# Second attention of a decoder layer: scores and contexts of two batches at once, as 64 by 64 products on quarters of the TensorE array

## What is computed

```python
x = x + xattn(layernorm(x), ctx_512)          # ctx_512: (32, 64, 64)

kv_r   = rope(kv_c)                           # (b, 64 keys, 64)
q_big  = rope(einsum('bshk,hkq->bshq', q, w_kc_q))
q_r    = einsum('bshq,hqr->bhsr', q_big, W_qr)
k_r    = einsum('bld,hdr->bhlr', kv_r, W_kr)
scores = einsum('bhsr,bhlr->bhsl', q_r, k_r)  # 16 heads, 64 by 64
attn   = softmax(scores)
ctx_c  = einsum('bhsl,bld->bhsd', attn, kv_r)
ctx    = einsum('bhsd,hkd->bhsk', ctx_c, w_kc_kv)
return ctx.reshape(b, s, H * K) @ Wo.T
```

## Time and profile before

| | us |
|---|---|
| median of 3 runs | 771.22 |
| the three runs | 771.22, 772.04, 767.51 |
| the profiled execution, in all | 763.03 |
| its span in the trace | 761.2 |
| mean granted clock of PE, as a share of full | 0.955 |

### The profile page before, as it was taken

How to read it: one execution, slowest core, us unless ns; L and a number is a source line. 1 busy time by engine, 2 the same in 40 slices (tenths; PEclk the granted TensorE clock), 3 DMA queues, 4 the chain that set the end, 5 groups by cost and what they waited for, 6 DMA issues and landing times.

```text
span 761.2 us, 13640 instructions
## 1 busy us (share of the span) xinstructions
PE 662.7 (87%) x4850; PEld 490.5 (64%) x4850; DVE 529.0 (69%) x1237; ACT 333.4 (44%) x1001; POOL 237.2 (31%) x219
## 2 busy tenths in 40 slices
PE   4787999989999889989899898998979797899780
PEld 2465777767785557856578465785656586788660
DVE  4998789994676868578794777846587746344472
ACT  0477789986721173011730117301366354444340
POOL 1131000000028423453446534465334001201554
PEclk9997899996999999999999999999999999999995
DMA  8799800000000000000000100001071133333545
GB/s 302 162 382 420 351 2 2 1 2 1 2 15 15 1 1 1 1 14 1 16 21 23 55 1 15 22 21 43 14 251 50 48 93 97 117 105 100 155 127 179
DMA packets 49905, 61.44 MB, mean 81 GB/s; under 512 B 15536, under 2 KB 42416, under 8 KB 49584
## 3 DMA queue, kind: packets, MB, share of 16 engines
q1 hardware_dynamic: 45104, 50.88, 20.1%
q0 software_dynamic: 3072, 8.39, 3.6%
q10 hardware_dynamic: 1664, 1.31, 0.6%
HBM read 29.37 MB, written 31.20 MB: 80 GB/s over the span
## 4 chain that ended last, share of the span: by engine, by line
PE 65%; DVE 14%; ACT 9%; issue 6%; POOL 3%; DMA 2%; another core or an unknown queue 1%; ACTq 0%; POOLq 0%; DVEq 0%
PE bank L348 55%; PE bank L357 9%; DVE m L1052 3%; ACT ex L1546 2%; POOL r L1701 2%; ACT kbd L1425 1%; DVE qmax L1264 1%; DVE wlo L1296 1%; ACT vbd L1411 1%; DMA lncol<-in_L_attn_ln_kv_b 1%; DVE csum L1273 1%; POOL gb L1753 1%; ACT ex L1435 1%; ACT xth L1391 1%
## 5 line engine op out<-in xcount | busy, mean ns | idle before, releaser
L1052 DVE TENSOR_TENSOR m<-bank,cst 128x512 f32<-128x512 f32 x192 | 118.8, 682 | 47.0 <-PE bank L348 46.2
L1701 POOL TENSOR_TENSOR r<-m,m 128x512 f32<-128x512 f32 x72 | 91.3, 1291 | 134.9 <-DVE m L1052 123.0
L348 PE MATMUL bank<-xth,wbh 128*128 128x512 f32 x192 | 83.4, 434 | 4.1 <-DVE m L1052 4.1
L348 PE MATMUL bank<-xth,wbl 128*128 128x512 f32 x192 | 75.1, 391 | 0.0
L348 PE MATMUL bank<-xtl,wbh 128*128 128x512 f32 x192 | 75.1, 391 | 0.0
L1534 ACT ACTIVATE qc<-bank 128x512 f32<-128x512 f32 x32 | 17.4, 595 | 128.8 <-PE bank L348 128.8
L1546 ACT ACTIVATE ex<-bank,nmax 128x64 f32<-128x64 f32 x256 | 56.1, 346 | 27.2 <-DVE nmax L1267 27.0
L348 PE MATMUL bank<-r,wqk 64*64 64x512 f32 x512 | 61.1, 621 | 1.7 <-POOL r L1701 1.7
L1721 POOL TENSOR_TENSOR ex<-ex,inv 128x512 f32<-128x512 f32 x32 | 33.3, 1042 | 82.7 <-DVE inv L1276 82.5
L348 PE MATMUL bank<-wop,qc 128*128 128x256 f32 x256 | 58.0, 379 | 0.6 <-DVE qc L1281 0.6
L348 PEld LDWEIGHTS bank<-wop,qc 128*128 128x128 f32 x256 | 48.5, 190 | 11.4 <-issue 4.3
(11 more groups left out here) (218 smaller groups left out, 1553.4 us busy)
## 6 DMA issues: line engine op xcount, KB each, us to landing
slots<-cst SPq DMA_DIRECT2D x1, 13312.0 KB, 44.2
xs<-slots SPq DMA_DIRECT2D x46, 128.0 KB
slots<-ys SPq DMA_DIRECT2D x46, 128.0 KB
slots<-cst SPq DMA_DIRECT2D x1, 5120.0 KB, 49.7
wo_s<-in_L_xattn_Wo SPq DMA_DIRECT2D x1, 2048.0 KB, 18.3
wq_s<-in_L_xattn_Wq SPq DMA_DIRECT2D x1, 2048.0 KB, 11.9
wraw<-in_L_ffn_Wg SPq DMA_DIRECT2D x8, 256.0 KB, 5.0
wraw<-in_L_ffn_Wu SPq DMA_DIRECT2D x8, 256.0 KB, 5.3
```

The costliest lines, as they stand in the source:

```text
L348: return e.matmul(o, l, r, start=start, stop=stop, skip_group_check=True)
L1052: last = e.tensor_tensor(m4[n % 2][m][:, :].rearrange("p (b s) -> p b s", s=S), products[half][:, :].rearrange("p (b s) -> p b s", s=S), t ...
L1701: last = e.tensor_tensor(rope[n % 6][half][:, :], m4[n % 2][first][:, :], m4[n % 2][second][:, :], op)
```

## The change

Scores. The block-diagonal keys are gone. POOL writes the rotated context straight into `kvr[blk % 2]` (two buffers now, 128 partitions by 8 batches by 64, the same 64 rows twice), and `context_T` turns it into `kvT` by 16 products with the identity, 64 by 64 by 64, once per block at n = 9, with one copy of 128x512 on ACT. `cross_scores` now makes two batches in 32 products of 64 by 64 by 64, each on a quarter of the array, into banks 4 and 5: heads with even number within `qc` rows 0 to 63 go to bank 4, the others to bank 5. So each bank holds half the heads of both batches; maximum, exponentials, sum, normalisation and transposes go on as before, eight times per block, on a bank each.

Contexts. Instead of one product of 128 by 128 by 512, `contexts` makes four of 64 by 64 by 256, for half the heads of two batches, into `context_banks`, banks 1 and 7. Both calls of a pair have to be done before DVE can copy a batch out, so `context_out` runs twice in steps 5, 7, 9 and 11. The heads end in a new order, which is made good by folding the output weights in that order (`context_head`, `outputs_T`, `outputs_fold`).

Banks. Since bank 1 now holds contexts and bank 3 the output products, the six tiles ahead all use banks 0 and 2, and tile n waits for c_rm of 12 blk + n, that is for DVE's products of tile n-1. The seventh tile waits for the last context copy and the last addition to x of the block before.

Order. `cross_scores` comes at s = 0, 2, 4, 6 at the head of the step; `AHEAD` moves the first three tiles one step forward; `norm_T` does two at a time at s = 0 and 1; `cross_out` comes at s = 7, 9, 11, 12.

```diff
-        AHEAD = {5: 0, 6: 1, 7: 2, 8: 3, 10: 4, 12: 5}
+        AHEAD = {4: 0, 5: 1, 6: 2, 8: 3, 10: 4, 12: 5}
...
-        out_bank = lambda blk, t: bank[4 + t % 2 if blk < 3 else t]
-        OUT_AT = [{9: 0, 10: 1, 11: 2, 12: 3}] * 3 + [{6: 0, 8: 1, 10: 2, 12: 3}]
+        out_bank = lambda blk, t: bank[3] if blk < 3 else bank[(0, 2, 3, 4)[t]]
+        OUT_AT = {7: 0, 9: 1, 11: 2, 12: 3}
+        context_banks = (bank[1], bank[7])
...
-            odd = (n + (blk == 0)) % 2
+            odd = 0 if blk and n < 6 else (n + 1) % 2
             return bank[odd], bank[2 + odd]
...
-                w.wait_ge(c_rm, 12 * blk + n - 1 if n > 1 else 12 * blk)
+                if blk and n < 6:
+                    w.wait_ge(c_rm, 12 * blk + n)
+                elif blk and n == 6:
+                    w.wait_ge(c_cn, 8 * blk)
+                    w.wait_ge(c_xc, 4 * blk)
+                else:
+                    w.wait_ge(c_rm, 12 * blk + n - 1 if n > 1 else 0)
...
-            def cross_scores(blk, b):
-                i = 8 * blk + b
+            def cross_scores(blk, d):
+
+                i = 8 * blk + 2 * d
                 w.wait_ge(c_qb, 8 * blk + 6)
-                w.wait_ge(c_kvT, 2 * (blk + 1))
-                w.wait_ge(s_ex, 32 + i - 1)
-                for n in range(NP):
-                    if n == 6:
+                w.wait_ge(c_kvT, blk + 1)
+                w.wait_ge(s_ex, 32 + i)
+                for n2 in range(4):
+                    if n2 == 3:
                         w.wait_ge(c_qb, 8 * (blk + 1))
-                    at = 64 * (n % 2)
-                    last = mm(e, bank[4 + b % 2][at:at + 64, (n // 2) * P:(n // 2 + 1) * P], qc[:, n, b * 64:(b + 1) * 64], kvbdT[:, b, :], True, True)
-                last.then_inc(s_S, 1)
+                    for b2 in range(2):
+                        b, at = 2 * d + b2, 256 * b2 + 64 * (n2 ^ b2)
+                        for odd in range(2):
+                            rows = slice(64 * odd, 64 * odd + 64)
+                            for c in range(2):
+                                last = mm(e, bank[4 + odd][64 * c:64 * c + 64, at:at + 64], qc[rows, 2 * n2 + c, b * 64:(b + 1) * 64], kvT[rows, b, :], True, True)
+                last.then_inc(s_S, 2)
...
             def contexts(blk, b):
                 i = 8 * blk + b
+                d, u = divmod(b, 2)
                 w.wait_ge(s_exs, 32 + i + 1)
-                w.wait_ge(c_cn, i)
+                w.wait_ge(c_cn, 8 * blk + 2 * d)
                 w.wait_ge(r_route, RK * blk)
-                mm(e, bank[7][:, :], kvbd[:, b, :], ssb[b % 2][:, :], True, True).then_inc(c_ctxv, 1)
+                for b2 in range(2):
+                    for s in range(2):
+                        rows, c = slice(64 * s, 64 * s + 64), s ^ b2
+                        last = mm(e, context_banks[b2][64 * c:64 * c + 64, 256 * u:256 * u + 256], kvr[blk % 2][rows, 2 * d + b2, :],
+                                  ssb[b % 2][rows, 256 * b2:256 * b2 + 256], True, True)
+                last.then_inc(c_ctxv, 1)
...
             def context_out(blk, b):
-                i = 8 * blk + b
-                w.wait_ge(c_ctxv, i + 1)
-                e.tensor_copy(qc[:, :, b * 64:(b + 1) * 64], bank[7][:, :].rearrange("p (n s) -> p n s", s=S)).then_inc(c_cn, 1)
+                w.wait_ge(c_ctxv, 8 * blk + b + 2 - b % 2)
+                e.tensor_copy(qc[:, :, b * 64:(b + 1) * 64], context_banks[b % 2][:, :].rearrange("p (n s) -> p n s", s=S)).then_inc(c_cn, 1)
...
-                    if 4 <= s < 12:
-                        context_out(blk, s - 4)
-                    if 1 <= s < 5 and blk < 3:
-                        norm_T(blk, s - 1)
-                    if s - 1 in OUT_AT[blk]:
-                        cross_out(blk, OUT_AT[blk][s - 1])
+                    if 5 <= s < 12 and s % 2:
+                        for b in (s - 5, s - 4):
+                            context_out(blk, b)
+                    if 1 <= s < 3 and blk < 3:
+                        for m in (2 * s - 2, 2 * s - 1):
+                            norm_T(blk, m)
+                    if s - 1 in OUT_AT:
+                        cross_out(blk, OUT_AT[s - 1])
...
-            def context_diag(blk):
-                w.wait_ge(c_kvr, blk + 1)
-                w.wait_ge(s_S, 16)
-                w.wait_ge(c_ctxv, 8 * blk)
-                w.wait_ge(c_kvTp, 2 * blk)
-                for h2 in range(2):
-                    last = e.tensor_tensor(kvbd[:, :, 64 * h2:64 * h2 + 64], kvr[:, :, :],
-                                           C("half")[:, h2:h2 + 1].rearrange("p (o d) -> p o d", o=1).broadcast_to([P, 8, XC]), ALU.mult)
-                last.then_inc(c_kvbd, 1)
```

More of the change, by code:

```diff
@@ L607, in outputs_T @@
                 w.wait_ge(s_oT, n)
-                transposes(e, [(bank[3][:, (h * 2 + t) * P:(h * 2 + t + 1) * P], wo_s[:, t, (2 * n + h) * P:(2 * n + h + 1) * P])
-                               for h in range(2) for t in range(2)]).then_inc(s_oTp, 1)
+                at = lambda s: P * context_head(n // 2, n % 2, s)
+                transposes(e, [(bank[3][:, (s * 2 + t) * P:(s * 2 + t + 1) * P], wo_s[:, t, at(s):at(s) + P])
+                               for s in range(2) for t in range(2)]).then_inc(s_oTp, 1)
             def outputs_fold(g):
@@ L1559, in norm_T @@
                 w.wait_ge(c_proj, 24 * (blk + 1))
-                e.activation(xth[:, k, 256 * half:256 * half + 256], bank[m % 2][:, 0:256], ACT.Copy).then_inc(s_xth, 1)
+                e.activation(xth[:, k, 256 * half:256 * half + 256], bank[2 * (m % 2)][:, 0:256], ACT.Copy).then_inc(s_xth, 1)
             def weights_high(n):
```

93 lines of the change are left out of this document (50 added, 43 removed).

## The result

The changed kernel took 815.2 us (median of four runs, 809.6 to 816.7) against 769.4 for the kernel before in the same session: a ratio of 1.0565, 95% interval 1.0496 to 1.0634, or 46 us more. The forecast was 23.6 us more, and 815.2 lies above its range. The profiled execution took 809.63 us, with a span of 807.8 (before: 761.2).

The account below looks back on a forecast made before the run. PE was taken to bound part two's second stretch, the scores-to-exponentials loop its first. The sum 5.3 + 2 x 6.4 - 0.5 + 6.0 = 23.6 us, added to the median 771.2, gave 794.8 us; range 781 to 809.

Parts of the forecast that it names:

- The waits of the tiles ahead: Part two's second stretch: PE waits 3.8, 3.2, 0.3 and 0.9 us before the second, third, sixth and seventh tile.
- The clock: Slow PE work behind new gaps, third gap counted as nothing: 2.0 us per block, 6.0 in all, between 0 and 15.
- if the clock's share is several times the 6 us: Sign named beforehand that the prediction is wrong: slow-clock loss far above the 6 us forecast.
- The first stretch: Part two up to the first tile ahead, paced by scores, maximum, exponentials: 0.9 us more in the first block.
- PE's saving: Part two after the first tile ahead (second stretch), first block: scores -1.1, contexts -2.5, transposes +0.6, so 3.0 us less.
- Contexts of 0.5 for six of 1.0: Second stretch: seven contexts on quarters at 0.5 us where six took 1.0, 2.5 us less PE work.
- The router's slots: DVE work of 2.1 us before the fourth maximum, delaying the third lot of scores: 1.1 us more in blocks two and three.
- The parts without the clock: Blocks one to three before any clock loss: 5.3 us more in the first, 6.4 each in the second and third.
- Fourth block: No tiles ahead; last context copy no longer late but the head slower: -0.5 us, between -2 and +2.
- Waits, but the clock holds: 789: Rival: the new waits come but PE keeps full clock, 17.6 us more, about 789; chance 0.14.
- The slow contexts: Rival: both row halves writing one bank keep contexts from running on four quarters at once, about 806; chance 0.14.
- PE's own work decides: Rival: less PE work outweighs the waits, 21 us saved, time falls to 750; chance of faster 0.07.

Follow-up runs that it names:

- e1_fill: Changed kernel with unneeded dummy products on PE in four gaps of part two, blocks one to three, no wait removed: ratio 1.0255 to the kernel before.
- e2_order: Changed kernel with DVE's products of the first two tiles ahead put before the context copies and the maximum: ratio 1.0233 to the kernel before.
- e7_sc128: Changed kernel with each lot of scores as 16 products of 128 rows by 64 columns, not on quarters: ratio 1.0687 to the kernel before.
- e3_ctx128: Changed kernel with each call's four context products replaced by two of 128 by 128 by 256, not on quarters: ratio 1.0507 to the kernel before.
- e5_after: The changed kernel itself, unaltered, run again in a later session beside other variants: ratio 1.0663 to the kernel before.
- e8_bankrow: Changed kernel with the context products laid so that each row half of the array writes its own bank: ratio 1.0581 to the kernel before.
- e4_serial: Kernel before with only the banks' part of the change, all six tiles ahead in banks 0 and 2: ratio 1.052 to the kernel before.

## Why the prediction was wrong

- **The waits of the tiles ahead: right.** 3.8, 3.2, 0.3 and 0.9 us were forecast ahead of the second, third, sixth and seventh tile, and 3.80, 3.03, 0.15 and 0.52 came, the same in all three blocks. No wait at the fourth and fifth, as said. The four together were 0.7 us shorter than forecast.
- **The clock: the step that failed.** "I take 1.0 us for each of the first two gaps and nothing for the third: 2.0 per block, 6.0 in all" was 25.6 us by `e1_fill` (23.6 with the second profile of the changed kernel), 20.8 (17.5) of them in part two, where the gaps stand: beyond even the 15 of its upper bound. The prediction had named this itself as a sign of being wrong, "if the clock's share is several times the 6 us". Two things were wrong in it. A slow stretch behind a gap falls wholly on work where PE is full and costs 1.5 to 1.7 us, as `e2_order` shows, and not 1.0. And I priced two gaps where there are four: the wait of the second pair of norm transposes for DVE's `xtl` (3.46 us, 3.09 in the later blocks) I never saw, because I followed the loop of scores alone, and the third of my gaps got nothing. Twelve gaps in three blocks at 1.5 to 1.7 us are 18 to 20 us, which is what part two lost. The first stretch grew from 15.35 to 17.89 us with the clock lost; that slow scores lengthen the loop through ACT in turn fits this, but no run parts it off.
- **PE's saving: wrong.** Of the term "-3.0" in the second stretch, nothing is left: 43.09 measured against 43.12 without any saving. Scores came out as forecast (1.16 for 1.1), and `e7_sc128` shows that the quarters are what makes them so. "Contexts of 0.5 for six of 1.0" failed: I took a context's length in the timeline for what it adds, but its neighbours overlap it before, and around the quarters they do not: from its start to the tile's it was 0.46 us and is now 0.60, and the stretch holds seven where it held six. In three blocks this is some 9 us. That it brings nothing `e3_ctx128` shows; that the overlap is the reason is read from the starts.
- **The first stretch:** +0.9 was forecast, +1.35 came with the clock kept (15.35 for 14.0), +3.9 without. The router's slots made the gap before the third lot 5.4 us in the later blocks for 4.0 in the first, 1.4 for the forecast 1.1; the later blocks' first stretches came to 16.7 us with the clock kept, 1.7 over the 15.0 of before, for the 2.0 forecast.
- **The parts without the clock, together:** forecast 5.3 + 2 x 6.4 = 18.1, by `e1_fill` 8.0 + 8.2 + 8.3 = 24.5. The 6.4 us between them are nearly the missing 3 x 3.0 less what the four waits were shorter than forecast, 3 x 0.7.
- **Fourth block:** -0.5 forecast, +2.8 came up to the experts' first products (50.10 us for 47.31). Its three gaps before lots of scores are 4.27, 5.36 and 2.16 us, the clock is 0.83, and the head of the part is later by more than the last copy gained.
- **The rivals.** "Waits, but the clock holds: 789" is what `e1_fill` builds: 1.0255 x 769.4 = 789. That the number agrees is luck in part, since the rival counts 9 us of PE's saving that did not come, and the clock of the fourth block is still low in `e1_fill`. The slow contexts were right in effect and wrong in reason: contexts saved next to nothing, but with one bank for both row halves and with a bank for each they take the same 0.60 us from start to start (`e5_after`, `e8_bankrow`). The Trainium skill's rule (TensorEngine Tiling (Array Packing), Restrictions and Gotchas) that different row tiles can't access one bank simultaneously did not show here, where the two row halves write different partition halves of it; the measurement decides. That PE's own work decides fell with its saving.

## What to carry to other kernels

A gap on a PE that was full can cost more than its length: look for every gap that a change makes, on all queues that PE waits for. Here a gap of 3 to 4 us cost 1.5 to 1.7 us more in most cases; where a gap can't be avoided, dummy products may keep the clock. What a PE operation costs is the distance from its neighbour's start to the next one's, not its length in the timeline, and an operation that changes the array's tiling may lose the overlap on both sides, as the contexts did here. PSUM banks that let two tiles be in flight were worth more here (1.052 without them) than a shorter product. And when a remedy is tried on the changed kernel, try it on the kernel before too: that is the comparison that says whether the change pays.

## What the runs showed that I had not expected

- Dummies alone made the kernel before 1.0% faster (interval 0.6 to 1.3%), with nothing else moved.
- The same gap can be followed by a slow stretch in one run and not in another: behind the same wait of 2.5 us the first block's router transposes took 1.09 us in the kernel before, and 1.93 in the changed one; in `e4_serial` waits of 3.72 us were followed by one and waits of 3.17 were not. What decides it was not settled.
- A lot of scores, 32 products of 64 by 64 on four quarters in 64 instructions, takes 1.09 us from start to start at full clock, 17 ns for an instruction, and 1.92 at the lower level.
